# Factorization machine on one core: the first half's input groups loaded in pairs with rows of 32 KB, and a pair's slots given back at the first product of its squares

## The reference, cut to what matters

```
emb         = x @ factors                       # x is 1024 x 12500, factors 12500 x 16
x_reg       = x @ W_lin.T + b_lin
sum_squared = square(emb.sum(axis=1))
squared_sum = (square(x) @ square(factors)).sum(axis=1)
h = relu(emb @ W1.T + b1);  h = relu(h @ W2.T + b2)       # 16 -> 128 -> 64
dnn = h @ W3.T + b3
y   = 0.5 + 5 * sigmoid(x_reg + 0.5 * (sum_squared - squared_sum) + dnn)
```

## Time and profile before

| | us |
|---|---|
| median of three runs | 134.65 |
| the profiled execution's own time | 134.6 |
| its span from first to last instruction | 132.4 |
| PE busy | 106.6 |
| ACT busy | 64.1 |
| DVE busy | 53.1 |
| POOL busy | 12.5 |

### The profile page before, as it was taken

One profiled execution on the slowest core, in us unless ns is written; L12 is line 12 of the kernel. 1 busy time (PEld: TensorE's weight loads), 2 busy tenths in 40 slices (PEclk: granted clock), 3 DMA queues, 4 the chain that ended last, 5 costly groups with the idle time before them and its releaser, 6 DMA issues.

```text
span 132.4 us, 2859 instructions
## 1 busy us (share of the span) xinstructions
PE 106.6 (81%) x1123; PEld 31.6 (24%) x1123; DVE 53.1 (40%) x51; ACT 64.1 (48%) x72; POOL 12.5 (9%) x48
## 2 busy tenths in 40 slices
PE   6089999768877877877978869996967966989992
PEld 4012222111111211211212312211111111335881
DVE  0392450532531541540540292450451351576571
ACT  4031660734733743742744394652662562465851
POOL 4016001110010011011011001151000000000000
PEclk9999999999999999999999999999999999999998
DMA  4999999999999999999999999999999999999800
GB/s 115 397 460 431 430 431 426 430 426 431 421 435 426 435 426 416 440 426 431 431 426 426 426 430 426 421 440 416 435 421 431 435 418 424 411 411 411 321 13 6
DMA packets 4639, 52.34 MB, mean 395 GB/s; under 512 B 532, under 2 KB 664, under 8 KB 1688
## 3 DMA queue, kind: packets, MB, share of 16 engines
q1 hardware_dynamic: 4632, 52.23, 93.6%
HBM read 52.22 MB, written 0.00 MB: 394 GB/s over the span
## 4 chain that ended last, share of the span: by engine, by line
DMA 63%; PE 28%; SPq 3%; ACT 3%; issue 2%; DVE 1%; ACTq 0%
DMA xr<-in_x_groups 52%; PE p_lin L467 22%; DMA xr<-in_x_end 11%; ACT sq L298 2%; PE p_sq L467 2%; PE p_h L557 2%; SPq L236 1%; PE p_tot L467 1%; PE p_h L588 1%; DVE h L419 0%; DVE h L414 0%; PE p_tot L570 0%; SPq L234 0%; SPq L233 0%; SPq L232 0%
## 5 line engine op out<-in xcount | busy, mean ns | idle before, releaser
L298 ACT ACTIVATE sq<-xr 128x1536 f32<-128x1536 f32 (+1 forms) x40 | 48.5, 1262 | 47.2 <-DMA xr<-in_x_groups 47.2
L394 DVE TENSOR_TENSOR sq<-xr 128x1536 f32<-128x1536 f32 x20 | 35.1, 1758 | 56.6 <-DMA xr<-in_x_groups 56.6
L467 PE MATMUL p_lin<-xr,wr 128*17 128x512 f32 x320 | 38.2, 594 | 13.8 <-DMA xr<-in_x_groups 13.8
L467 PE MATMUL p_lin<-sq,wz 128*18 128x512 f32 x320 | 38.2, 594 | 2.3 <-ACT sq L298 1.0
L467 PEld LDWEIGHTS p_lin<-xr,wr 128*17 128x17 f32 x320 | 7.9, 97 | 42.3 <-issue 21.6
L467 PEld LDWEIGHTS p_lin<-sq,wz 128*18 128x18 f32 x320 | 8.2, 97 | 31.5 <-ACT sq L298 16.9
L273 POOL COPY wr<-hd x20 | 7.4, 372 | 71.5 <-PE p_lin L467 70.8
L402 DVE TENSOR_TENSOR sq<-xr 128x320 f32<-128x320 f32 (+5 forms) x15 | 10.4, 724 | 8.1 <-DMA xr<-in_x_end 8.1
L307 ACT ACTIVATE sq<-xr 128x320 f32<-128x320 f32 (+5 forms) x15 | 9.1, 652 | 7.1 <-DMA xr<-in_x_end 7.1
L467 PE MATMUL p_lin<-xr,hd 128*17 128x352 f32 (+1 forms) x128 | 10.0, 380 | 1.5 <-DMA xr<-in_x_end 1.5
L467 PE MATMUL p_lin<-sq,ws 128*18 128x352 f32 x64 | 6.6, 459 | 0.0
(11 more groups left out here) (50 smaller groups left out, 34.7 us busy)
## 6 DMA issues: line engine op xcount, KB each, us to landing
xr<-in_x_groups SPq DMA_DIRECT2D x20, 2048.0 KB, 15.4
xr<-in_x_end SPq DMA_DIRECT2D x1, 2112.0 KB, 10.8
xr<-in_x_end SPq DMA_DIRECT2D x3, 640.0 KB, 12.3
xr<-in_x_end SPq DMA_DIRECT2D x1, 1760.0 KB, 14.6
xr<-in_x_end SPq DMA_DIRECT2D x1, 1056.0 KB, 12.7
hd<-in_head SPq DMA_DIRECT2D x1, 952.0 KB, 4.8
xr<-in_x_end SPq DMA_DIRECT2D x1, 704.0 KB, 14.1
xf<-in_x_first SPq DMA_DIRECT2D x1, 512.0 KB, 5.7
```

Source lines behind the costliest of these rows:

```text
L298: nc.scalar.activation(sq[:, s, c:c + n, :], xr[:, s, c:c + n, :], ACT.Square).then_inc(act_squared, 1)
L394: nc.vector.tensor_tensor(sq[:, s, 0:BY_DVE, :], xr[:, s, 0:BY_DVE, :], xr[:, s, 0:BY_DVE, :], ALU.mult).then_inc(dve_squared, 1)
L467: return nc.tensor.matmul(out, lhsT, rhs, start=False, stop=False, skip_group_check=True)
```

## The change

The first half's 12 groups become 6 pairs. A pair is one DMA of 128 rows of 32 KB, 4 MB in all, into two neighbouring slots of the ring; in HBM it has rows of `PAIR_PITCH` = 8192 + 64 floats. One semaphore, that of the pair's even slot, tells that both groups have landed. The second half's groups stay single.

PE works through a pair as multiply, multiply, squares, squares. It waits for the squares of both groups at once, and the first product of the pair's squares raises a new semaphore, `x_used`, by two; SP waits for that before it loads the next pair. `sq_used` still rises at the last product of each group, and still guards `sq`, `wr` and `wz`, and the second half's loads in `xr`.

```
+TWO = 2
+PAIR_PITCH = TWO * CHUNKS * HALF + 64
...
+        def landed(engine, r, s, h):
+            if h == 0:
+                engine.wait_ge(x_landed[s - s % TWO], 16 * (r + 1))
+            elif s % TWO == 0:
+                engine.wait_ge(x_landed[s], 16 * (r + 1))
+            else:
+                engine.wait_ge(x_landed[s], 16 * (r + (1 - ROUNDS[0])))
...
-            for s in range(RING):
-                sp.dma_start(xr[:, s].rearrange("p c b -> p (c b)"), x_groups[s, :, 0:CHUNKS * HALF]).then_inc(x_landed[s], 16)
-            with sp.Fori(1, sum(ROUNDS)) as r:
+            for t in range(RING // TWO):
+                sp.dma_start(xr[:, TWO * t:TWO * t + TWO].rearrange("p s c b -> p (s c b)"),
+                             x_pairs[t, :, 0:TWO * CHUNKS * HALF]).then_inc(x_landed[TWO * t], 16)
+            with sp.Fori(1, ROUNDS[0]) as r:
+                for t in range(RING // TWO):
+                    sp.wait_ge(x_used, RING * r + (TWO * t + TWO - RING))
+                    sp.dma_start(xr[:, TWO * t:TWO * t + TWO].rearrange("p s c b -> p (s c b)"),
+                                 x_pairs[bass.ds(RING // TWO * r + t, 1), :, 0:TWO * CHUNKS * HALF]
+                                 .rearrange("g p n -> (g p) n")).then_inc(x_landed[TWO * t], 16)
+            with sp.Fori(ROUNDS[0], sum(ROUNDS)) as r:
                 for s in range(RING):
                     sp.wait_ge(sq_used, RING * r + s + 1)
                     sp.dma_start(xr[:, s].rearrange("p c b -> p (c b)"),
-                                 x_groups[bass.ds(RING * r + s, 1), :, 0:CHUNKS * HALF].rearrange("g p n -> (g p) n")
-                                 ).then_inc(x_landed[s], 16)
+                                 x_groups[bass.ds(RING * r + (s - GROUPS), 1), :, 0:CHUNKS * HALF]
+                                 .rearrange("g p n -> (g p) n")).then_inc(x_landed[s], 16)
...
             def add_squares(r, s, h):
                 g = RING * r + s
                 pe.wait_ge(wz_ready, g + 1)
-                pe.wait_ge(dve_squared, g + 1)
-                pe.wait_ge(act_squared, len(BY_ACT) * g + 1)
+                if h == 1:
+                    pe.wait_ge(dve_squared, g + 1)
+                    pe.wait_ge(act_squared, len(BY_ACT) * g + 1)
+                elif s % TWO == 0:
+                    pe.wait_ge(dve_squared, g + TWO)
+                    pe.wait_ge(act_squared, len(BY_ACT) * (g + TWO))
                 for c in range(BY_DVE + BY_ACT[0]):
-                    add_mm(quad(p_lin[h], c, WZ, 0, HALF), wz[:, s, c, :], sq[:, s, c, :])
-                pe.wait_ge(act_squared, len(BY_ACT) * g + 2)
+                    mm = add_mm(quad(p_lin[h], c, WZ, 0, HALF), wz[:, s, c, :], sq[:, s, c, :])
+                    if h == 0 and s % TWO == 0 and c == 0:
+                        mm.then_inc(x_used, TWO)
+                if h == 1:
+                    pe.wait_ge(act_squared, len(BY_ACT) * g + 2)
...
             with pe.Fori(0, ROUNDS[0]) as r:
-                for s in range(RING):
-                    multiply(r, s, 0)
-                    add_squares(r, s, 0)
+                for t in range(0, RING, TWO):
+                    for s in range(t, t + TWO):
+                        multiply(r, s, 0)
+                    for s in range(t, t + TWO):
+                        add_squares(r, s, 0)
```

More of the change, by code:

```diff
@@ L33 @@
 W_END = ALL - ENDS
-assert GROUPS % RING == 0 and (ALL - 1) % CHUNKS == 0 and END_GROUPS == RING
+assert RING % TWO == 0 and GROUPS % RING == 0 and (ALL - 1) % CHUNKS == 0 and END_GROUPS == RING
 REST_K = 32
@@ L79, with fm_kernel @@
 HD = HD_L + REST_SETS * LIN
-def fm_kernel(nc, head, x_first, x_rest, x_groups, x_end, out):
+def fm_kernel(nc, head, x_first, x_rest, x_pairs, x_groups, x_end, out):
     with ExitStack() as ctx:
@@ L146, in fm_kernel @@
         dve_squared = sem("dve_squared")
+        x_used = sem("x_used")
         sq_used = sem("sq_used")
@@ L290, in _, with squares @@
             nc.scalar.activation(sqf[:, :], xf[:, :], ACT.Square).then_inc(first_squared, 1)
-            def squares(r, s):
-                act.wait_ge(x_landed[s], 16 * (r + 1))
+            def squares(r, s, h):
+                landed(act, r, s, h)
                 act.wait_ge(sq_used, RING * r + s + 1)
@@ L330, in _ @@
                 for s in range(RING):
-                    squares(r, s)
+                    squares(r, s, 0)
             act.wait_ge(sq_used, RING + GROUPS)
@@ L342, in _ @@
                 for s in range(RING):
-                    squares(r, s)
+                    squares(r, s, 1)
             square_end(0, 0)
@@ L388, in _, with squares @@
             nc.vector.tensor_tensor(sql[:, :, :], xl[:, :, :], xl[:, :, :], ALU.mult).then_inc(rest_squared, 1)
-            def squares(r, s):
-                dve.wait_ge(x_landed[s], 16 * (r + 1))
+            def squares(r, s, h):
+                landed(dve, r, s, h)
                 dve.wait_ge(sq_used, RING * r + s + 1)
@@ L506, in multiply @@
             def multiply(r, s, h):
-                pe.wait_ge(x_landed[s], 16 * (r + 1))
+                landed(pe, r, s, h)
                 pe.wait_ge(wr_ready, RING * r + s + 1)
@@ L684 @@
     chunks = xT[P + REST:].reshape(ALL - 1, P, B)
-    x_groups = np.zeros((TOTAL, P, PITCH), f32)
-    for g in range(TOTAL):
-        h, c = g // GROUPS, CHUNKS * (g % GROUPS)
-        x_groups[g, :, :CHUNKS * HALF] = chunks[c:c + CHUNKS, :, h * HALF:(h + 1) * HALF].transpose(1, 0, 2).reshape(P, -1)
+    x_pairs = np.zeros((GROUPS // TWO, P, PAIR_PITCH), f32)
+    for g in range(GROUPS):
+        at = g % TWO * CHUNKS * HALF
+        x_pairs[g // TWO, :, at:at + CHUNKS * HALF] = \
+            chunks[CHUNKS * g:CHUNKS * (g + 1), :, :HALF].transpose(1, 0, 2).reshape(P, -1)
+    x_groups = np.zeros((TOTAL - GROUPS, P, PITCH), f32)
+    for g in range(TOTAL - GROUPS):
+        x_groups[g, :, :CHUNKS * HALF] = \
+            chunks[CHUNKS * g:CHUNKS * (g + 1), :, HALF:].transpose(1, 0, 2).reshape(P, -1)
     ends = chunks[ALL - 1 - ENDS:]
@@ L711 @@
     params[:, C_B3] = np.asarray(L0_rec_b3)
-    arrays = {"head": head, "x_first": x_first, "x_rest": x_rest, "x_groups": x_groups, "x_end": x_end}
+    arrays = {"head": head, "x_first": x_first, "x_rest": x_rest, "x_pairs": x_pairs, "x_groups": x_groups, "x_end": x_end}
     nc = bacc.Bacc("TRN2", target_bir_lowering=False, num_devices=1)
```

## The result

The changed kernel takes 139.44 us (median of four runs, 138.84 to 140.91) against 134.62 for the kernel before: a ratio of 1.0375, with a 95% interval of 1.0286 to 1.0463. I had forecast 134.2, in a range of 133.9 to 134.9. The kernel is 4.8 us slower, and its runs now differ by 2 us, where those of before agree within 0.1.

A forecast was written before the change was run, and what follows sets the result against it. The prediction took the DMA input stream as the bound, with PE having some air. From 134.6 us it took off 0.43 for six pairs and added 0 for refills and the rest: 134.17, given as 134.2, range 133.9 to 134.9.

The forecast's parts named there:

- Part 1: First half's loads: six 4 MB transfers for twelve of 2 MB save 0.071 us each, 0.43 us in all.
- the same line: Part 1's fit of time against bytes through end pieces and groups: 434.9 GB/s, leaving 0.071 us a transfer.
- nothing changes: Rival on the input stream: cost is per byte, or rows are cut into the same packets; 134.65 us, chance 0.22.
- Part 2: Refill of the ring by pairs: issued 4.2 us before the other pair lands, so no gap at four refills.
- need of 1.5 to 2.5 us: Latency of a transfer into an empty queue, bounded by the last output store and the first load.
- T: Moment a pair lands; squares' first product forecast at T + 4.94, SP's next issue at about T + 5.5.
- Part 3: Change of halves: thin margins at groups 12, 14 and 16; refills cost 0, upper bound 0.1 us.
- T4: Landing of the first of the last two pairs; group 12's load forecast to be issued at T4 + 6.9.
- T5: Landing of the last pair; loads of groups 14 and 16 forecast at T5 + 6.9 and T5 + 17.2.
- The ring runs dry at the change of halves: Rival: leads at groups 12, 14 and 16 too short; costs 1.1 us if 3.5 us are needed, 135.3; chance 0.07.
- Rows of 32 KB run worse: Rival: long rows and their HBM pitch slow the first half by 0.8 us, to 135.4 us; chance 0.04.
- The second fetch on a late engine: Rival: another instruction fetch on a DMA engine already behind costs 1.2 us, giving 135.4 us; chance 0.05.

The follow-up runs named there:

- even version: Changed kernel, SP waiting directly for PE's last multiplication and DVE's and ACT's squares, each pair's second group squared 4 and 4 by DVE and ACT: 134.89 us.
- fewer squares: Changed kernel, but ACT squares 2 of its 5 chunks per group in the first half, PE's work kept the same: 136.98 us.
- a lead of 4.1 us: Kernel before, first-half refills held until the first product of the group two before has begun: 140.34 us.
- run with a lead of 2.2: Kernel before, first-half refills held until the first product of the squares of the group two before: 147.2 us.
- run with 16 KB rows: Changed kernel, each pair loaded by two DMAs of 16 KB rows issued together, engines still waiting for both: 139.28 us.
- direct-release run: Changed kernel, SP waiting directly for PE's last multiplication and the squares of DVE and ACT, in both halves: 135.80 us.

## Why the prediction was wrong

**Part 1, the gain of 0.07 us a pair: right in size.** 9.72 us a pair with 3775 packets, in the even version; in the changed kernel itself late refills hide it. That a cost of each row or transfer goes, and not something of the place in HBM, fits; which of the two it belongs to no run tells. The size is in part luck. I took 107.07 and 125.35 for landings, but they are the starts of ACT and DVE, 0.10 and 0.02 us behind them. From the landings, 106.97 and 125.33, the same line gives 0.096 us a transfer. By the landings the first end piece also takes 5.03 us (106.97 to 112.00), as the sum has it, so what spoke for "nothing changes" was not there.

**Part 2, the refill of the pairs: wrong, and this is the step that failed.** The prediction set the need of 1.5 to 2.5 us against the landing of the other pair, "4.2 us before the other pair lands". The need was about right; the lead was not, for two reasons.
- The lead is to be counted to the moment at which the *first* DMA engine runs out, and a landing is the *last* of 16. In this kernel they are 1.4 to 3.0 us apart from the first refill on, and I had a part of the cause among my own rows: the long interval at 23.84 and the fetch beside it. I took it for a rival that might happen again, and not for something that shortens every lead by 1.2 us or more.
- The issue comes 6.2 us behind a landing and not 5.5. The squares' products start at T + 5.0 as forecast (38.18 to 43.19), but the first one is through and seen by SP only 1.05 us later, and the issue follows after 0.15: I had put 0.6 for both.

So the lead over the first engine was 9.72 - 1.8 - 6.2 = 1.7 us by this sum, under the need of some 2 us that the table below shows, where I saw 4.2. The four refills measured 3.1, 1.7, 2.6 and 0.7.

**Part 3, the change of halves: the places were right, the price wrong by the same step.** Groups 12, 14 and 16 were issued at T4 + 7.1, T5 + 7.1 and T5 + 17.5, against 6.9, 6.9 and 17.2 in my sum. Measured from the first engine that leaves 1.0, 0.9 and 1.3 us, and they cost about 2.2 us together with group 13 behind group 12. PE was level again from group 17 on, and the end pieces were not late.

**The rivals.** "The ring runs dry at the change of halves" is the one that came true, but with 0.07 of the chance, with a price of 1.1 us, and with the pairs themselves left out. Against it I had written that no row shows a need above 2.5. The need was not the mistake: it came out at about 2 us for the first engine. The lead was what I had overestimated. "Rows of 32 KB run worse" is refuted: rows of 16 KB did not help, and the even version runs at 9.72 us a pair with rows of 32 KB. The second fetch on a late engine did not happen in the first half: the first interval is 11.2 us against 11.0 before. It did happen in the end pieces, for 0.5 us, and not for 1.2. For row pitches at large powers of two the Trainium skill (DMA: Bandwidth & Descriptors, Latency and other measured facts) lists lower rates, 164 GB/s at 2 MiB and 103 at 4 MiB, against 214 at 4 MiB with a pad of 4 KiB. A pitch of 32 KB + 256 B is far from these, and the even version shows no loss with it.

**Open.** When only the first engines run out, the last one often loses as well, up to 2.0 us, though by its own lead of 3.1 to 3.6 us it should not. The trace shows that packets are long then: of the 768 packets of 32 KB the median takes 1.21 us, but the 14 begun from 56.5 to 57.75 us, behind the refill issued at 56.12, take 1.69 on average and up to 2.17. That engines which start again together get in each other's way would fit; no run tells it from another cause. Packets of up to 2.3 us also stand at 26.4 to 27.8 us, where the refill had a lead of 3.1 us over the first engine. So of the 4.8 us, the 2.0 that the last engine loses at pair 3 are tied to a short lead by the runs, but how they come about is not shown. Open too is why the runs of the versions with thin leads differ by 2 to 4 us.

## What to carry to other kernels

This stream was full only while every DMA engine had work, and the landing that a profile shows is that of the last engine. Before a change makes transfers larger in a ring of the same size, take the issue of each refill from the trace, subtract it from the landing ahead, subtract the spread of the engines (the 16 increments of the semaphore), and ask that 3 us are left, from which on loads of 2 and 4 MB lost nothing to speak of here. And a signal "at the first product" comes when that product is through, some 1.05 us after it starts here; when a slot is held by two other engines as well, let the issuer wait for these directly.

## What the runs showed of the hardware

Taken over 172 refills of twelve kernels (one profiled execution each; the runs with fewer squares and with a lead of 4.1 us are left out), by the lead over the first engine:

```
lead over the      refills   lost by the first engine   lost by the last engine
first engine, us             mean (from .. to)          mean (from .. to), us
below 1               9      1.71 ( 0.80 .. 5.46)       1.26 ( 0.00 .. 3.10)
1.0 to 1.5            6      0.75 ( 0.48 .. 0.94)       0.83 ( 0.01 .. 1.99)
1.5 to 2.0            4      0.66 ( 0.46 .. 1.00)       1.48 ( 0.95 .. 2.02)
2.0 to 2.5            5      0.50 ( 0.26 .. 1.06)       0.35 (-0.03 .. 0.86)
2.5 to 3.0            7      0.10 (-0.01 .. 0.42)       0.19 (-0.15 .. 0.84)
3.0 to 4.0           28      0.04 (-0.01 .. 0.24)       0.00 (-0.16 .. 0.08)
4.0 and more        113      0.00 (-0.07 .. 0.11)       0.03 (-0.08 .. 1.24)
```

Where the lead is 1 us or less, lead and loss of the first engine add up to 1.8 to 2.0 us, also for the one refill issued 3.5 us too late. So to an engine with nothing to do a refill costs some 2 us on top of the time of its data. From 3 us of lead on the first engine loses at most 0.24 us. The 1.24 us of the last engine in the bottom row stand beside a packet of the instruction queue (at 89.66 us, in the run with a lead of 2.2). The Trainium skill (DMA: Bandwidth & Descriptors, Anatomy of one DMA) has 2.0 us for the part of a DMA that does not depend on its size, for another kind of queue; the runs agree.

TensorE's granted clock was at its lower level of 1.2 GHz for a time behind pauses of 2.67 and 3.23 us in the changed kernel, not behind one of 2.11; in the run with 16 KB rows it fell behind one of 1.98 too. The length of the pause alone does not tell: the clock stayed up behind 2.72 us in the direct-release run and behind 2.92 in the run with a lead of 2.2. Before the change, with pauses of 1 us, it stayed at 2.4 GHz. Behind a fall 32 multiplications took 5.1 to 5.3 us in place of 3.6, with part of them already at the higher level.
